# Moving the last block's routing into the experts' program, on one Trainium2 core

## The reference

```python
probs = softmax(xf @ Wg); topv, topi = top_k(probs, 2)
gates = topv / sum(topv)
oh  = one_hot(topi.reshape(-1), e)
pos = sum(cumsum(oh, axis=0) * oh, axis=-1) - 1     # place in the expert's queue
keep = pos < cap                                     # cap = 1076
buf[eidx * cap + pos] = x                            # scatter, e * cap slots
h = gelu(expert_in @ W1 + b1); y = h @ W2 + b2
out = sum over the two choices of gate * y           # gather
```

## Time and profile before

| | us |
|---|---|
| median of 3 runs (1307.44 to 1310.98) | 1310.62 |
| the profiled execution | 1314.12 |
| its span, first to last instruction | 1312.4 |
| busy: PE | 1162.6 (89%) |
| busy: ACT | 919.0 (70%) |
| busy: DVE | 633.8 (48%) |
| busy: POOL | 354.6 (27%) |

### The profile page before, as it was taken

How to read it: one execution, slowest core, us unless ns; L and a number is a source line. 1 busy time by engine, 2 the same in 40 slices (tenths; PEclk the granted TensorE clock), 3 DMA queues, 4 the chain that set the end, 5 groups by cost and what they waited for, 6 DMA issues and landing times. The chain is left out here.

```text
span 1312.4 us, 24491 instructions
## 1 busy us (share of the span) xinstructions
PE 1162.6 (89%) x8759; PEld 495.6 (38%) x8759; DVE 633.8 (48%) x1767; ACT 919.0 (70%) x1203; POOL 354.6 (27%) x382
## 2 busy tenths in 40 slices
PE   7899999999999998999898889516999999999990
PEld 4322222222222222221222111114877877777770
DVE  4534342232546253625252301264687677677756
ACT  2799999999999897988798989215354354445414
POOL 2422112020131312312131300033535534544430
PEclk9999999999999998999898979857999999999995
DMA  6942422223231221213120100335135333422216
GB/s 152 195 104 67 94 67 70 58 73 100 60 107 53 94 66 44 78 49 89 36 81 9 38 3 7 122 106 173 22 108 125 49 98 107 92 45 29 27 21 256
DMA packets 83745, 104.22 MB, mean 79 GB/s; under 512 B 14937, under 2 KB 68932, under 8 KB 83632
## 3 DMA queue, kind: packets, MB, share of 16 engines
q1 hardware_dynamic: 66512, 77.74, 21.0%
q0 software_dynamic: 15744, 23.83, 8.7%
q10 hardware_dynamic: 1376, 1.18, 0.7%
HBM read 56.99 MB, written 48.29 MB: 80 GB/s over the span
## 5 line engine op out<-in xcount | busy, mean ns | idle before, releaser
L1358 ACT ACTIVATE prob<-ps_s 128x1024 f32<-128x1024 f32 (+3 forms) x854 | 719.3, 972 | 73.8 <-PE ps_s L1259 62.9
L1276 PE MATMUL ps_o<-prob,v_aug 128*17 128x512 f32 (+3 forms) x3294 | 436.2, 577 | 7.6 <-POOL prob L1384 2.9
L1259 PE MATMUL ps_s<-qop,kop 51*128 51x512 f16 (+3 forms) x1647 | 269.3, 374 | 39.6 <-ACT prob L1358 27.1
L1259 PEld LDWEIGHTS ps_s<-qop,kop 51*128 51x128 f16 x1647 | 63.1, 93 | 419.8 <-ACT prob L1358 381.9
L2109 PE MATMUL ps_y<-w2s,hs 128*128 128x256 bf16 (+1 forms) x1728 | 189.1, 273 | 1.1 <-DVE yb L2194 1.1
L2090 PE MATMUL ps_h<-xs,w1s 128*128 128x384 bf16 (+1 forms) x1152 | 181.7, 317 | 5.0 <-ACT hid L2156 4.3
L1384 POOL TENSOR_SCALAR_AFFINE_SELECT prob<-prob 128x256 f32<-128x256 f32 (+1 forms) x180 | 69.5, 397 | 418.2 <-ACT prob L1358 415.7
L2156 ACT ACTIVATE hid<-ps_h,b 128x384 f32<-128x384 f32 (+1 forms) x192 | 105.1, 560 | 109.9 <-PE ps_h L2090 86.0
L1420 DVE COPY acc<-ps_o 32x512 f32<-32x512 f32 (+2 forms) x105 | 72.1, 687 | 220.5 <-PE ps_o L1276 204.3
L2109 PEld LDWEIGHTS ps_y<-w2s,hs 128*128 128x128 bf16 (+1 forms) x1728 | 157.6, 99 | 18.3 <-DVE yb L2194 1.5
L2047 POOL DMA_INDIRECT result<-y,entry x72 | 111.7, 1551 | 175.7 <-DVE y L2199 142.1
(11 more groups left out here) (163 smaller groups left out, 731.7 us busy)
## 6 DMA issues: line engine op xcount, KB each, us to landing
w<-in_W SPq DMA_DIRECT2D x16, 1024.0 KB, 7.5
slots_x<-empty POOLq DMA_DIRECT2D x12, 520.0 KB, 4.1
qop<-fparts_q SPq DMA_DIRECT2D x42, 128.0 KB, 4.2
xe<-slots_x SPq DMA_DIRECT2D x8, 650.0 KB
x_all<-in_xT SPq DMA_DIRECT2D x8, 512.0 KB, 4.8
attnT<-acc SPq DMA_DIRECT2D x128, 32.0 KB
aT<-attnT SPq DMA_DIRECT2D x16, 256.0 KB
x_all<-in_x SPq DMA_DIRECT2D x8, 512.0 KB
```

The lines of the kernel that those rows point to most:

```text
L1259: mm = pe.matmul(ps_s[:, u.p % SLOTS_S, e, a.q0:], o.key(e, a.h, a.kt), o.query(e, a.h, a.b, a.q0), start=True, stop=True)
L1276: mm = pe.matmul(ps_o[32 * c:32 * c + VW, a.q0:], o.v[:, a.kt, a.h], prob[:, t % RING, c % 2, c // 2, a.q0:], start=a.first, stop=a.last)
L1358: act.activation(prob[:, t % RING, n, e:z, q0:], ps_s[:, u.p % SLOTS_S, e:z, q0:], ACT.Exp, scale=1.0 / (SCALE * SCALE)).then_inc(exp_done, 1)
```

## The change

`route_last` is gone. Block 7's routing becomes a class `Last`, whose methods are the first thing that each engine does in the program of `experts`.

- Heads 8 to 15 of block 7, complete by turn 400, are loaded from DRAM at turn 401 (`EARLY_TURN`), and scaled in turns 405 to 408. The residual is loaded at turn 380 (`FLAG_TURN`).
- Heads 0 to 7 go by DMA from `acc` straight to `aT` and `total` in SBUF (`take_last`), with an address from the flag's register. In the last turn SP does head 3 and ACT head 1. `load_general` loads the same data from DRAM in the flag's general case, and otherwise fills a place that nothing reads.
- `scale_last` does one half of the heads at a time. PE multiplies heads 8 to 15 for all 4 tiles first, then adds heads 0 to 7 tile by tile, each tile in its own PSUM bank.
- The root of the variance runs between the steps of the choice; the choice works on logits that aren't multiplied by the root. ACT normalises the rows and takes the high parts a tile at a time; DVE takes the low parts.
- PE runs 40 matmuls whose results nothing reads (256 columns, f32) from the counts on until after the last scatter.
- The low parts of expert 0's weights go from POOL to DVE, after the last scatter's issue. SP itself waits for the scatters to land, and loads the first experts' rows.

```diff
-LOAD_AT[BLOCK_END[NB - 1]] = NB - 1
+EARLY_TURN = max(j.end + LAG for j in JOBS if any(b == NB - 1 and h >= H // 2 for _, b, h in j.heads)) + 1
+EARLY_SCALE_AT = {EARLY_TURN + 4 + _s: _s for _s in range(KT)}
...
+    def take_last(r, eng, f, h, rows, total, signal):
+        n = NB - 1
+        eng.dma_start(r.aT[h * DH:(h + 1) * DH, bass.ds(1 - f, 1), 0], rows.unsqueeze(1)).then_inc(signal, 16)
+        eng.dma_start(r.total[h * DH:h * DH + 1, bass.ds(2 * f, 1)], total.unsqueeze(1)).then_inc(signal, 16)
+    def scale_last(r, dve, c, s):
+        n = NB - 1
+        u, cols = n % 2, slice(s * P, (s + 1) * P)
+        step = (1 - c) * KT + s
...
+        den = r.den[:, s % 2, c:c + 1]
+        dve.stream_shuffle(den, r.total[:, c:c + 1, cols], [0] * DH + [DH] * DH).then_inc(r.spread, 1)
+        dve.wait_ge(r.spread, n * KT + step + 1)
+        dve.reciprocal(den, den).then_inc(r.inverted, 1)
+        dve.wait_ge(r.inverted, n + step + 1)
+        dve.tensor_tensor(r.aT[:, u, c:c + 1, cols], r.aT[:, u, c:c + 1, cols], den, ALU.mult).then_inc(r.scaled, 1)
...
-def route_last(nc, io, psum, r, x):
...
+class Last:
+    def sync(l, sp, x, io):
+        r = l.r
+        x.load_weights(sp, io, 0, 0)
+        x.load_constants(sp, io)
+        x.load_weights(sp, io, 1, 1)
+        r.store_base(sp, l.N)
+        sp.wait_ge(r.scattered, NB * KT * 2 * 16)
+    def tensor(l, pe, out, count, warm):
+        r, u = l.r, l.N % 2
+        for c in (1, 0):
+            for s in range(KT):
+                if c == 0 or s == 0:
+                    pe.wait_ge(r.scaled, l.BASE + (KT if c == 1 else KT + s + 1))
+                mm = pe.matmul(out[:, s, 0:D + E], r.aT[:, u, c, s * P:(s + 1) * P], r.wp[:, c, :], start=(c == 1), stop=(c == 0))
+                if c == 0:
+                    mm.then_inc(r.y_mm, 1)
+        r.pe_count(pe, l.N, count[:, 0:KT * E])
+        for m in range(2 * KT + 1):
+            if m >= 1:
+                pe.wait_ge(l.issued, m)
+            for _ in range(10 if m == 0 else 3 if m < 2 * KT else 9):
+                pe.matmul(warm[:, 0:QB // 2], r.aT[:, u, 0, 0:P], r.aT[:, u, 0, 0:QB // 2], start=True, stop=True)
...
+    def vector(l, dve, out, count, x):
+        r, n = l.r, l.N
+        dve.wait_ge(r.last_loaded, 48)
+        for k, stored in enumerate(stores_until(N_STEPS)):
+            dve.wait_ge(l.out_stored[k], stored)
+        for s in range(KT):
+            r.scale_last(dve, 0, s)
+            if s >= 1:
+                r.dve_tile(dve, n, s - 1, out[:, s - 1])
+                l.stats(dve, s - 1)
...
+        roots = l.roots(dve)
+        for _ in l.choices(dve):
+            next(roots, None)
...
+        for s in range(KT):
+            dve.wait_ge(r.split_high, n + s + 1)
+            dve.tensor_tensor(r.low[:, s], r.x1[:, n % 2, s], r.high[:, s], ALU.subtract).then_inc(r.split_low, 1)
+        dve.wait_ge(l.issued, 2 * KT + 1)
+        for k in range(2):
+            x.weights_low(dve, 0, 0, k)
+    def scalar(l, act, x):
+        r, n = l.r, l.N
+        for k in range(2):
+            x.weights_high(act, 0, 0, 0, k)
+        act.wait_ge(l.root, RSQRT_STEPS + 1)
...
+        for s in range(KT):
+            act.activation(r.x1[:, n % 2, s], r.x1[:, n % 2, s], ACT.Identity, scale=r.rstd[:, s:s + 1],
+                           bias=l.nmr[:, s:s + 1]).then_inc(r.x1_done, 1)
+            if s == 0:
                 r.act_gate(act, n)
...
+            act.wait_ge(r.x1_done, n * KT + s + 1)
+            act.activation(r.high[:, s], r.x1[:, n % 2, s], ACT.Identity).then_inc(r.split_high, 1)
+    def gpsimd(l, pool):
+        r, n = l.r, l.N
+        for m in range(2 * KT):
...
+            pool.wait_ge(r.split_low, n + m // 2 + 1)
+            alone(pool)
+            r.scatter_rows(pool, n, m, r.scattered)
+            pool.sem_inc(l.issued, 1)
+        pool.memset(l.done[:], 0.0).then_inc(l.issued, 1)
```

More of the change, by code:

```diff
@@ L295, with stores_until @@
 assert FLAG_TURN < BLOCK_END[NB - 1]
-LOAD_AT[BLOCK_END[NB - 1]] = NB - 1
+EARLY_TURN = max(j.end + LAG for j in JOBS if any(b == NB - 1 and h >= H // 2 for _, b, h in j.heads)) + 1
+EARLY_SCALE_AT = {EARLY_TURN + 4 + _s: _s for _s in range(KT)}
+assert FLAG_TURN < EARLY_TURN and max(EARLY_SCALE_AT) < N_TURNS
+assert all(j.end + LAG > FLAG_TURN for j in JOBS for _, b, h in j.heads if b == NB - 1 and h < H // 2)
+def stores_until(end):
+    return [max([j.stores for j in JOBS if j.number % ACCS == k and j.end <= end], default=0) for k in range(ACCS)]
 PIECES = sorted(PIECE_AT)
@@ L1192, in _ @@
                         a = job.number % ACCS
-                        for c, b, h in job.heads:
+                        for i, (c, b, h) in enumerate(job.heads):
                             cols, row = slice(b * QB, (b + 1) * QB), 32 * c
+                            if b == NB - 1 and h < H // 2:
+                                if t < N_TURNS - 1 or i % 2 == 0:
+                                    r.take_last(sp, f, h, acc[row:row + DH, a], acc[row + DH:row + VW, a], out_stored[a])
+                                continue
                             sp.dma_start(attnT[h * DH:(h + 1) * DH, cols], acc[row:row + DH, a]).then_inc(out_stored[a], 16)
@@ L1772, in places, with place_rows @@
     def places(r, dve, n, bank):
-        c = r.chain
+        r.place_rows(dve, r.chain, n, bank)
+        r.chain.end()
+        r.weigh(dve, n)
+    def place_rows(r, dve, c, n, bank):
         dve.wait_ge(r.c_mm, n + 1)
@@ new lines, with __init__, stats, roots @@
+class Last:
+    N = NB - 1
+    BASE = (NB - 1) * KT
+    def __init__(l, r, out_stored, sb, sem):
+        l.r, l.out_stored = r, out_stored
+        l.nmr = sb("last_nmr", [P, KT], F32)
+        l.drop = sb("last_drop", [P, KT], F32)
+        l.done = sb("last_done", [1, 1], F32)
+        l.stats_done = sem("last_stats")
+        l.choice = sem("last_choice")
+        l.root = sem("last_root")
+        l.issued = sem("last_issued")
+    def sync(l, sp, x, io):
[20 more added lines that the diff above has]
+                pe.matmul(warm[:, 0:QB // 2], r.aT[:, u, 0, 0:P], r.aT[:, u, 0, 0:QB // 2], start=True, stop=True)
+    def stats(l, dve, s):
+        r = l.r
+        dve.wait_ge(r.summed, l.BASE + s + 1)
+        dve.bn_stats(r.stats[:, s], r.x1[:, l.N % 2, s]).then_inc(l.stats_done, 1)
+    def roots(l, dve):
+        r = l.r
+        c = Chain(dve, l.root, 0, RSQRT_STEPS + 1)
+        yield from rsqrt_pieces(c, r.mv[:, :, 1], [r.tmp[:, k] for k in range(5)], r.rstd[:])
+        c.wait()
+        c.did(dve.scalar_tensor_tensor(out=l.nmr[:], in0=r.mv[:, :, 0], scalar=-1.0, in1=r.rstd[:], op0=ALU.mult, op1=ALU.mult))
+        c.end()
+        yield
+    def choices(l, dve):
+        r = l.r
+        c = Chain(dve, l.choice, 0, 2 + 2 * KT + 4 + KT - 2)
+        l.chain = c
+        mean = r.mv[:, :, 0:1].broadcast_to([P, KT, E])
+        c.did(dve.tensor_tensor(r.shiftl[:], mean, r.wsum[:].unsqueeze(1).broadcast_to([P, KT, E]), ALU.mult))
+        yield
+        c.wait()
+        dve.wait_ge(r.logits_out, NB * KT)
+        c.did(dve.tensor_tensor(r.clogit[:], r.slogit[:], r.shiftl[:], ALU.subtract))
+        yield
+        c.wait()
+        for s in range(KT):
+            c.did(dve.max(r.top[:, s], r.clogit[:, s]))
+            yield
+        c.wait()
+        for s in range(KT):
+            c.did(dve.max_index(r.topi[:, s], r.top[:, s], r.clogit[:, s]))
+            yield
+        c.wait()
+        c.did(dve.tensor_copy(r.chosen[:], r.topi[:, :, 0:2]))
+        yield
+        c.wait()
+        c.did(dve.tensor_tensor(r.hot[:], r.iota[:], r.chosen[:].unsqueeze(3).broadcast_to([P, KT, 2, E]), ALU.is_equal))
+        yield
+        c.wait()
+        c.did(dve.tensor_tensor(r.counts[:], r.hot[:, :, 0], r.hot[:, :, 1], ALU.add))
+        yield
+        c.did(dve.tensor_copy(r.ahead[:, 0], r.run[:]))
+        yield
+        for s in range(1, KT):
+            c.wait()
+            ahead = dve.tensor_tensor(r.ahead[:, s], r.ahead[:, s - 1], r.counts[:, s - 1], ALU.add)
+            if s < KT - 1:
+                c.did(ahead)
+            else:
+                ahead.then_inc(r.count_done, 1)
+            yield
+        c.end()
+    def vector(l, dve, out, count, x):
[8 more added lines that the diff above has]
+                l.stats(dve, s - 1)
+        r.dve_tile(dve, n, KT - 1, out[:, KT - 1])
+        l.stats(dve, KT - 1)
+        dve.wait_ge(l.stats_done, KT)
+        for s in range(KT):
+            dve.bn_aggr(r.mv[:, s], r.stats[:, s]).then_inc(l.stats_done, 1)
+        dve.wait_ge(l.stats_done, 2 * KT)
+        roots = l.roots(dve)
+        for _ in l.choices(dve):
+            next(roots, None)
+        for _ in roots:
+            pass
+        dve.tensor_tensor(l.drop[:], r.top[:, :, 1], r.top[:, :, 0], ALU.subtract).then_inc(l.stats_done, 1)
+        dve.wait_ge(l.stats_done, 2 * KT + 1)
+        dve.tensor_tensor(r.gap[:, n % 2], l.drop[:], r.rstd[:], ALU.mult).then_inc(r.gap_done, 1)
```

(24 more changed lines are left out.)

160 lines of the change are left out of this document (76 added, 84 removed).

## The result

The changed kernel's median is 1295.45 us (1289.89 to 1297.27, 4 runs), beside 1310.8 for the kernel before on the same chip: ratio 0.9868, 95% interval 0.9841 to 0.9896, so faster by 17.3 us (13.6 to 20.8). The forecast was 25.1 faster, and its range ended at 1293. So the direction held and the size didn't; some 8 us are to be found.

The account below looks back on a forecast made before the run. The routing between attention and experts, up to the load of expert 0's rows, was taken to bound the kernel; 9.3 + 9.1 + 4.2 - 0.4 + 1.0 + 2.4 - 0.5 = 25.1 us gained, from 1310.6 to 1285.5, range 1280.5 to 1293.

Parts of the forecast that it names:

- a wait that I don't see: Remaining case, no place named: an unseen wait leaves the time about unchanged; chance 0.02.
- (g): Idle matmuls queued on PE ahead of the first expert's transposes: 0.5 us lost (0 to 6).
- (e): Last scatter to the load of expert 0's rows, SP itself waiting for the landing: 1.0 us gained.
- the first rival: Before the transposes: the queue of idle matmuls sets their start, 5.2 us after the rows, 1290; chance 0.12.
- (b): Block 7's scaling, residual and statistics, at half width and without a slowed multiply: 9.1 us gained (7.5 to 10.5).
- The clash that the change removes: In the routing, DVE's multiply took 4.10 us, not 0.42, beside POOL taking W1's low part; 3.7 counted as gained.
- (a): Last attention copy to first scaling, five loads from DRAM removed: 9.3 us gained (8.5 to 10).
- (c): Root, choice and places up to the first scatter: 4.2 us gained (2.2 to 5.2).
- (f): PE's clock in the first expert, already at 2.4 GHz: 2.4 us gained (0 to 2.4).
- ACT wasn't late: Rival before the first scatter: ACT late with the high parts, 4 us lost, 1289.5; chance 0.08.
- (d): The eight scatters, the first beside DVE's low-part subtractions: 0.4 us lost (0 to 2.5).
- The scalings brought forward: Rival at the attention's tail: the four early scalings aren't free, costing 6 us, 1291.5; chance 0.05.

Follow-up runs that it names:

- experiment 2: Changed kernel without the 40 idle matmuls, run in two groups; ratios to the kernel before 0.9839 and 0.9828.
- experiment 4: Changed kernel with each idle matmul replaced by four semaphore increments on PE; ratio to the kernel before 0.9922.
- experiment 5: Changed kernel with 22 semaphore increments added behind each tile's second product, 88 instructions more ahead of the loop; ratio to the kernel before 0.9848.
- experiment 6: Changed kernel with 18 idle matmuls of 512 columns in place of 40 of 256; ratio to the kernel before 0.9871.
- experiment 8: Kernel before with 42 tiny matmuls (168 PE instructions) added behind the last routing's count products; ratio to the kernel before 1.0026.
- experiment 10: Changed kernel with 35 idle matmuls and 27 tiny matmuls where PE waits anyway, moving the loop on; ratio to the kernel before 0.9823.
- experiment 1: Changed kernel and kernel before run again, nothing edited; ratios to the kernel before 0.9863 and 0.9985.
- experiment 3: Changed kernel with the attention as before: block 7's heads through DRAM, no early loads or scalings; ratio to the kernel before 0.9995.
- experiment 9: Kernel before with the low part of expert 0's W1 moved from POOL in the routing to DVE in the experts' program; ratio 0.9988.
- experiment 7: Changed kernel with the weights' low parts not held back until the last scatter is issued; ratio to the kernel before 0.9855.

## Why the prediction was wrong

**The step that failed** is the first sentence on what sets the end: that whatever brings the load forward "brings the end forward by the same time, as long as the experts' stage is left as it is". Its text was left as it is; its place in PE's instruction stream wasn't. This costs 4.2 us in the profiled execution (over all seven with it 4.2 to 4.7 where the clock falls behind the stand, 2.9 and 3.3 where it doesn't), and no term, rival or sign in the prediction stood for it but "a wait that I don't see", 0.02. Experiments 2, 4, 5, 6, 8 and 10 show the cause from both sides: it comes with 72 (experiment 6) or 160 instructions ahead of the loop, matmuls or increments alike, and with 168 in the kernel before, and goes with none or 248. The trace of the kernel before could have warned of the price: the flag's branch had it, 3.42 us with PE standing for 3.05. With the stand alone, 25.1 becomes 20.9.

**(g) was mis-sized.** The idle matmuls cost 1.1 to 2.4 us and not 0.5. In the first profiled execution their speed was right (19.1 us for the 40 on PE's timeline, where 19.4 was forecast), but the load was issued 0.5 earlier than forecast, and what (e) gained so was lost in the queue. In experiment 1 they took 20.39: the clock was low for their first 5.8 us, against 3.3. That is the first rival, which had 0.12, at a fraction of its price of 5.

**(b) rested on one execution of the kernel before.** The clash that the change removes took 3.68, 1.29 and 3.60 us in the three executions seen; the sum counted 3.7 as if it were always there. That is 0.8 too much by the mean of the three, and 2.4 by the smallest.

**The attention's end** was forecast as unmoved, and in the profiled pair it came 4.5 later. Experiment 3 undoes everything that the change puts beside the attention and doesn't get it back. On the chip of experiment 1 the last copy came at 800.7 in the kernel before and at 802.4 to 804.5 in three with the change or most of it; on that of experiments 8 to 10 at 802.6 and 803.2, and at 800.9 and 804.6. The means differ by 2.7 and by -0.1. On the chip of experiments 4 to 7 four kernels whose attention is the changed kernel's to the letter had their last copy at 835.4, 835.5, 838.3 and 843.2. So executions alone can differ by more than the 4.5, and whether 1 to 2 us of it belong to the change stays open.

Together: 25.1, and 0.8 for the wait in the second expert; less 4.2, 0.6 to 1.9, 0.8, and 0 to 2.7. That makes 16.3 to 20.3, where 17.3 (13.6 to 20.8) was measured.

**What was right.** (a), (b) as to its widths, (c), (e) and (f) came out within 0.7 us each. ACT wasn't late: it had split the weights by 854.84 and then waited 2.19 us for DVE. (d) was 0 and not 0.4: the 0.42 us subtraction that fell into the first scatter left it at 0.99, while a longer one does stretch scatters, as the earlier trace rows said and experiment 7 shows. The scalings brought forward cost nothing that shows (experiment 3). The clock stood at 1.00 when the first expert began. And both signs of being wrong that were given, transposes that begin well after the rows have landed and a last copy that moves, did appear, though neither is the stand.

## What to carry to other kernels

Instructions put ahead of a loop can cost time inside it. When a stage that wasn't edited gets longer, look in the chain for an "issue" without a releaser at the loop's turn, at how long the branch took, and at the count of instruction fetches; then move the loop with a few instructions in an idle place and measure again. Work that only keeps the clock up stands in its engine's queue, and where it outlasts the data's arrival it gives back what it gains: here the kernel without it is as fast as any. And before a removed clash is counted at its traced price, see it in more than one execution.

## What the runs showed of the hardware

- **A turn back of 3.3 to 3.8 us.** In seven executions the branch of the loop's only turn back took 3.31 to 3.79 us and PE stood for 2.43 to 2.92 of them, with 76 instruction fetches of 16 KB in the run; in the seven others, with 66 or 67 fetches, it took 0.24 to 0.25 and PE didn't stand. The Trainium skill ("Advanced Engine Details and Errata", section "Control Flow Timing") gives a compare-and-branch about 108 ns. Measured is 0.24 to 0.25 us for the turn back without a refetch, 0.08 for the same branch where it doesn't turn back, and with a refetch 30 times the page's figure and more. In each of the seven a packet of the instruction queue starts 0.98 to 1.02 us after the slow branch does, and none follows the fast ones for over 95 us; that the branch waits for just this packet is the plain reading and wasn't tested apart. By the trace's count, 0 and 248 instructions more ahead of the loop are free, 72 and 160 aren't, nor are 168 in the kernel before. One pass of the loop has some 1709 PE instructions, and a packet came for about every 250, so by its place the loop lies on seven packets or on eight. That seven are kept and eight aren't would fit all the runs; no run tests it.
- **Subtractions with both inputs in SBUF hold scatters up.** Two of 2.3 us beside them made scatters of 2.52 and 1.90 us out of 0.98. The inference in the Trainium skill ("SBUF — State Buffer", section "Who interferes with whom") that such an operation leaves descriptor generation alone doesn't carry over to these scatters. Whether it fails isn't shown, here or in the earlier trace rows: a scatter also reads its row numbers, `dest_all`, from SBUF, and no run parts the two. How long the overlap is matters: one of 0.42 us did nothing.
- **Increments of a semaphore on PE take 0.15 us each**, 22 of them about 3.2 us, so they are no cheap filler.
